# Batch 6's product with w made in fp32 between the counts and the matrix, and the matrix made by chunks

## The reference

```python
h = jnp.maximum(_layernorm(x, axis=-1), 0.0)           # x: (64, 128, 1024)
xp = jnp.transpose(h, (2, 0, 1)); n = 1024              # node, batch, feature
x_avg = xp.mean(axis=1)
x_norm = x_avg / jnp.maximum(norm(x_avg), 1e-12)
sim_flat = ((x_norm @ x_norm.T + 1.0) * 0.5).reshape(-1)
adj = (sim_flat + gumbel[:, 0] > 1.0 - sim_flat + gumbel[:, 1])   # n x n, 0 or 1
adj_sym = clip(adj + adj.T, 0, 1); nmask = clip(adj_sym + eye(n), 0, 1)
common = nmask @ nmask.T                                # the counts
struct = where(adj_sym * (common > 1) > 0, common / common.max() * common, 0)
W = adj * struct
dinv = where(W.sum(0) > 0, W.sum(0) ** -0.5, 0)
Wn = dinv[:, None] * W * dinv[None, :]                  # the matrix
xw = einsum('nbt,to->nbo', xp, weight)                  # each batch's product with w
out = x + transpose(einsum('sd,sbt->dbt', Wn, xw) + bias)
```

## Time and profile before

| | |
|---|---|
| median of 3 runs | 814.52 us (813.65 to 814.91) |
| profiled execution, its own time | 813.88 us |
| profiled execution, its span | 811.9 us |
| busy: PE, DVE, ACT, POOL | 97%, 68%, 62%, 37% |
| granted TensorE clock | 1.00 |

### The profile page before, as it was taken

One profiled execution on the slowest core, in us unless ns is written; L12 is line 12 of the kernel. 1 busy time (PEld: TensorE's weight loads), 2 busy tenths in 40 slices (PEclk: granted clock), 3 DMA queues, 4 the chain that ended last, 5 costly groups with the idle time before them and its releaser, 6 DMA issues.

```text
span 811.9 us, 14245 instructions
## 1 busy us (share of the span) xinstructions
PE 789.5 (97%) x5042; PEld 445.7 (55%) x5042; DVE 553.4 (68%) x668; ACT 502.3 (62%) x530; POOL 304.4 (37%) x389
## 2 busy tenths in 40 slices
PE   5999999899999999999999999999999999999998
PEld 5887766644455545554555455545555555545553
DVE  7999877999966656665666566656665666566653
ACT  4999966695665656655656565556664666566641
POOL 4667482103333333333333333333333333333320
PEclk9999999999999999999999999999999999999999
DMA  8999942005742223322322232223222322232112
GB/s 328 408 409 410 418 183 77 2 0 209 256 155 99 97 99 108 106 95 97 111 99 98 92 118 94 94 96 114 92 101 95 112 93 97 96 111 96 52 47 85
DMA packets 30126, 112.68 MB, mean 139 GB/s; under 512 B 3472, under 2 KB 3600, under 8 KB 29072
## 3 DMA queue, kind: packets, MB, share of 16 engines
q1 hardware_dynamic: 30096, 112.28, 38.0%
HBM read 78.71 MB, written 33.55 MB: 138 GB/s over the span
## 4 chain that ended last, share of the span: by engine, by line
PE 82%; DVE 3%; ACT 3%; issue 2%; POOL 1%; DMA 0%; POOLq 0%; DVEq 0%; ACTq 0%; SPq 0%
PE ps L998 67%; PE ps L915 8%; PE ps L1014 3%; PE ps L933 2%; DVE xring L1178 1%; ACT zbuf L492 1%; PE ps L785 1%; DVE a L1222 0%; ACT a L687 0%; PE ps L807 0%; PE ps L868 0%; DVE ybuf L1215 0%; ACT zbuf L561 0%; POOL zbuf L465 0%; DVE hring L1204 0%
## 5 line engine op out<-in xcount | busy, mean ns | idle before, releaser
L998 PE MATMUL ps<-a,ybuf 128*128 128x512 f16 x2604 | 570.8, 379 | 0.6 <-ACT obuf L598 0.3
L998 PEld LDWEIGHTS ps<-a,ybuf 128*128 128x128 f16 x2604 | 252.5, 98 | 296.4 <-issue 0.8
L1215 DVE TENSOR_TENSOR ybuf<-zbuf,ybuf 128x1024 f16<-128x1024 f32 x124 | 165.1, 1332 | 154.3 <-ACT ybuf L580 154.3
L463 POOL TENSOR_TENSOR zbuf<-zbuf 128x512 f32<-128x512 f32 x31 | 39.5, 1275 | 423.4 <-ACT zbuf L561 423.4
L580 ACT ACTIVATE ybuf<-zbuf 128x1024 f16<-128x1024 f32 x124 | 117.7, 950 | 114.3 <-POOL zbuf L468 98.9
L598 ACT ACTIVATE obuf<-ps,bias_sb,w_out 128x512 f32<-128x512 f32 x61 | 47.1, 772 | 111.9 <-PE ps L998 109.5
L1204 DVE TENSOR_TENSOR hring<-hring 128x1024 f16<-128x1024 f32 x53 | 67.0, 1264 | 54.7 <-ACT hring L539 54.7
L915 PEld LDWEIGHTS ps<-w,hring 128*128 128x128 f16 x1272 | 75.3, 98 | 12.6 <-issue 0.8
L915 PE MATMUL ps<-w,hring 128*128 128x128 f16 x1272 | 79.7, 219 | 0.3 <-DVE k L1248 0.3
L1374 DVE TENSOR_TENSOR obuf<-obuf,xring 128x1024 f32<-128x1024 f32 x63 | 77.2, 1226 | 2.7
L561 ACT ACTIVATE zbuf<-ps 128x1024 f32<-128x1024 f32 x55 | 56.3, 1023 | 22.0 <-PE ps L915 20.2
(11 more groups left out here) (164 smaller groups left out, 665.1 us busy)
## 6 DMA issues: line engine op xcount, KB each, us to landing
xring<-in_x_dram SPq DMA_DIRECT2D x96, 512.0 KB, 4.7
out_dram<-obuf SPq DMA_DIRECT2D x63, 512.0 KB, 2.9
ybuf<-in_x_dram SPq DMA_DIRECT2D x28, 512.0 KB, 11.9
a<-in_L_gnn_gumbel_dram SPq DMA_DIRECT2D x7, 1024.0 KB, 19.0
obuf<-in_x_dram SPq DMA_DIRECT2D x10, 512.0 KB, 6.0
obuf<-in_L_gnn_gumbel_dram SPq DMA_DIRECT2D x1, 1024.0 KB, 26.3
out_dram<-obuf SPq DMA_DIRECT2D x2, 256.0 KB, 2.1
w<-in_adj_dram SPq DMA_DIRECT2D x1, 64.0 KB, 1.9
```

Source lines behind the costliest of these rows:

```text
L998: mm = nc.tensor.matmul(bank[q % 2], y16[:, q % 2, yk, u, c * P:(c + 1) * P], a16[:, ak, mat, c, :], start=(start and c == yk == ak == 0), ...
L1215: nc.vector.tensor_tensor(y16[:, q % 2, 1, a:a + n, :], z[:, a + 1:a + 1 + n, :], y16[:, q % 2, 0, a:a + n, :], ALU.subtract).then_inc(s_y, 1)
```

## The change

1. Batch 6 is made as 4 and 5 are: `relu_first(6)` and `first_xw(6)`. `relu2(0, 3, 0)`, `h_low(0, 3, 0)` and `xw_of(0, 3, 0)` go.
2. Batch 4 goes to PSUM pair 3, batch 5 to pair 0, batch 6 to pair 3 again, once `z_of(0, 2, 0)` has read batch 4. The copy L675 goes; `z_of` reads the PSUM pairs, batch 4's before the first `square` and batch 5's behind it, not after the matrix. The eight matmuls of 4 and 5 are laid between `squared`, `q_row` and `turn`.
3. `y_low(0, 1, 2)` and `y_low(0, 1, 3)` go from VectorE to GpSimd, ahead of `roots`. `z_sums(2)` moves ahead to where `s_alo` reaches 10, the end of the parts of the first pair.
4. The first block of the matrix is handed over in four chunks of 128 rows instead of two of 256. `square` no longer scales; instead `high` scales by `kappa2` (kappa squared) and `low` multiplies and subtracts in one instruction. `top_of(1)` and the kappa steps stand behind one and two `rooted`.
5. L1332 waits for `first_xw(6)` and stands behind the last `low_part`, not before it. `partial(0, 2, 1)` stands ahead of `z_of(0, 3, 0)`; `partial(0, 2, 2)` waits for one store, `upper1(0, 2)` for the other.

The diff, cut to its core:

```diff
+        ps_early = {4: pair[3], 5: pair[0], 6: pair[3]}
-        EARLY = (1, 4, 5)
+        EARLY = (1, 4, 5, 6)
# GpSimd
             z_sums(1)
+            for g in (2, 3):
+                a, n = GROUPS[g]
+                pool.wait_ge(s_yhi, 4 + g + 1)
+                pool.wait_ge(s_y, 4 + 4 + g)
+                nc.gpsimd.tensor_tensor(y16[:, 1, 1, a:a + n, :], z[:, a + 1:a + 1 + n, :], y16[:, 1, 0, a:a + n, :],
+                                        ALU.subtract).then_inc(s_y, 1)
             roots(0, 0, HC)
             roots(1, HC, C)
-            with pool.Fori(2, TRIPS * PAIRS) as r:
+            pool.wait_ge(s_alo, 10)
+            z_sums(2)
+            with pool.Fori(3, TRIPS * PAIRS) as r:
# ScalarE
             relu_first(5)
-            act.wait_ge(s_xw2, 6)
-            nc.scalar.activation(xw_res[:, 0, :], ps_xw2, ACT.Copy).then_inc(s_spill, 1)
+            relu_first(6)
+            z_of(0, 2, 0)
-                nc.scalar.activation(r, r, ACT.Square, scale=kappa[:, 0:1]).then_inc(s_a32, 1)
+                nc.scalar.activation(r, r, ACT.Square).then_inc(s_a32, 1)
-                nc.scalar.activation(a16[:, 0, mat, :, :], src, ACT.Copy).then_inc(s_ahi, 1)
+                nc.scalar.activation(a16[:, 0, mat, :, :], src, ACT.Identity, bias=0.0,
+                                     scale=kappa2[:, 0:1]).then_inc(s_ahi, 1)
+            square(rows_hi, 0, 0, 0)
+            z_of(0, 2, 1)
+            square(rows_hi, 0, 0, 1)
+            act.wait_ge(s_kap, 4)
+            high_rows(0, 0, rows_hi, 0, 0, 1)
+            high_rows(0, 0, rows_hi, 0, 1, 2)
+            for c in (2, 3):
+                square(rows_hi, 0, 0, c)
+                high_rows(0, 0, rows_hi, 0, c, c + 1)
-            relu2(0, 3, 0)
-            z_of(0, 2, 0)
-            z_of(0, 2, 1)
             y_high(0, 2, 0)
# TensorE
+            pe.wait_ge(s_z, 4)
             for half in (0, 1):
+                first_xw(4, half, half + 1)
                 squared(C - 1, half).then_inc(s_diag, 1)
-            pe.wait_ge(s_z, 4)
-            first_xw(4).then_inc(s_xw2, 1)
-            stay_awake(ps[:, 1, 0:P], 2)
+            first_xw(4, 2).then_inc(s_xw2, 1)
+            first_xw(5, 0, HC)
             q_row(0)
+            first_xw(5, HC, HC + 2)
             turn(1)
+            first_xw(5, HC + 2).then_inc(s_xw2, 1)
             spread(1)
             q_row(1)
-            pe.wait_ge(s_spill, 1)
-            first_xw(5).then_inc(s_xw2, 1)
+            pe.wait_ge(s_z, 5)
+            first_xw(6).then_inc(s_xw2, 1)
                 product(1, 5, 5, ps_b, False)
-                xw_of(0, 3, 0)
                 pe.wait_ge(s_c, 14)
# VectorE
-            y_low(0, 1, 2)
             mask(5)
-            y_low(0, 1, 3)
             root(1, HC, C)
-            top_of(1)
             rooted(rows_hi, 0, 0, 0)
+            top_of(1)
+            rooted(rows_hi, 0, 0, 1)
...
+            nc.vector.tensor_tensor(kappa2[:], kappa[:], kappa[:], ALU.mult).then_inc(s_kap, 1)
+            rooted(rows_hi, 0, 0, 2)
+            rooted(rows_hi, 0, 0, 3)
+            low_part(0, 0, rows_hi, 0, 0)
+            low_part(0, 0, rows_hi, 0, 1)
+            rooted(rows_hi, 0, 1, 0)
+            low_part(0, 0, rows_hi, 0, 2)
+            rooted(rows_hi, 0, 1, 1)
+            low_part(0, 0, rows_hi, 0, 3)
...
+            low_part(3, 2, rows_lo, 1, 1)
+            dve.wait_ge(s_xw2, 8)
             nc.vector.tensor_tensor(spare, rows_hi[:, :, HI], rows_hi[:, :, LO], ALU.subtract).then_inc(s_t, 1)
-            low_part(3, 2, rows_lo, 1, 1)
-            h_low(0, 3, 0)
             low(4, 3, spare)
```

More of the change, by code:

```diff
@@ L118, in gnn_kernel @@
         kappa = sb("kappa", [P, 1])
+        kappa2 = sb("kappa2", [P, 1])
         w_out = sb("w_out", [P, 1])
@@ L601, in act_pair @@
             def act_pair(i, q, ahead1, ahead2):
+                first_loop = isinstance(i, int) and i == 0 and q == 2
                 partial(i, q, 0)
+                if first_loop:
+                    partial(i, q, 1)
                 if ahead1:
@@ L605, in act_pair @@
                     y_high(i, q + 1, 0)
-                partial(i, q, 1)
+                if not first_loop:
+                    partial(i, q, 1)
                 if ahead2:
@@ L693, in first_out, with high_rows @@
                                      scale=w_out[:, 0:1]).then_inc(s_first, 1)
-            for n, (mat, rows, k, half) in enumerate(((0, rows_hi, 0, 0), (A12, rows_hi, 0, 1),
-                                                      (1, rows_lo, 1, 0), (2, rows_lo, 1, 1))):
-                for part in (0, 1):
[L698 to L703, removed]
+            def high_rows(n, mat, rows, half, a, b):
+                act.wait_ge(s_a32, HC * n + b)
+                nc.scalar.activation(a16[:, 0, mat, a:b, :], rows[:, a:b, half * H:(half + 1) * H],
+                                     ACT.Identity, bias=0.0, scale=kappa2[:, 0:1]).then_inc(s_ahi, 1)
+            square(rows_hi, 0, 0, 0)
[7 more added lines that the diff above has]
+                high_rows(0, 0, rows_hi, 0, c, c + 1)
+            for n, (mat, rows, k, half) in enumerate(((A12, rows_hi, 0, 1), (1, rows_lo, 1, 0), (2, rows_lo, 1, 1))):
+                for part in (0, 1):
+                    square(rows, k, half, 2 * part)
+                    square(rows, k, half, 2 * part + 1)
+                    high_rows(n + 1, mat, rows, half, 2 * part, 2 * part + 2)
             act.wait_ge(s_wout, 1)
             act.wait_ge(s_bias, 16)
-            act.wait_ge(s_fh, 2)
+            act.wait_ge(s_fh, 3)
             first_out(0)
             first_out(1)
-            relu2(0, 3, 0)
             act.wait_ge(s_t, 1)
@@ L795, in _, with first_xw @@
             kept(TRIPS1 - 1, KEPT[1])
[L797 to L801, removed]
+            def first_xw(j, a=0, b=C):
+                pe.wait_ge(s_fh, j - 3)
+                for c in range(a, b):
+                    mm = nc.tensor.matmul(ps_early[j][:, c * P:(c + 1) * P], first_h[j][:, c * P:(c + 1) * P], w_unit[:],
                                           start=True, stop=True, skip_group_check=True)
@@ L1011, in first_pair @@
                             bank = FIRST_OUT[2 * (k % 2) + b][2]
-                            for c in (2 * part, 2 * part + 1):
+                            for c in cs:
                                 for yk, ak in ((0, 0), (0, 1), (1, 0)):
@@ L1017, in first_pair @@
                                                           skip_group_check=True)
-                            if part == 1 and k + b > 0:
+                            if cs[-1] == HC - 1 and k + b > 0:
                                 mm.then_inc(s_mm, 1)
@@ L1360, in upper1 @@
                 if isinstance(r, int) and r == 1:
-                    dve.wait_ge(s_hhi, 4)
+                    dve.wait_ge(s_hhi, before(0, BODY - 1) + 1)
+                if isinstance(r, int) and r == 2:
+                    dve.wait_ge(s_store[1], 32)
                 dve.wait_ge(s_mm, 14 + 7 * r + (6 if isinstance(r, int) and r == 1 else 5))
```

61 lines of the change are left out of this document (28 added, 33 removed).

## The result

| | before | after |
|---|---|---|
| median, 12 executions each on one chip | 814.48 us (813.51 to 815.42) | 815.91 us (814.65 to 816.89) |
| profiled execution, its own time | 813.88 us | 816.52 us |
| profiled execution, its span | 811.9 us | 814.7 us |

A forecast was written before the change was run, and what follows sets the result against it. TensorE was taken to bound the kernel: product(2, 5, 5) starts at 209.4 against 209.05, 0.35 us later, so 813.88 becomes 814.2, and 0.64 for the median gives 814.9. Own range 813.4 to 816.2; 8 in 10: 812.1 to 816.6.

The forecast's parts named there:

- End of the counts: Before the first product: powers 0.37 us earlier, q's maximum at about 149.8 for 150.3, GpSimd's two residues costing nothing.
- The rival in which the residues hold the masks: GpSimd's two residues keep masks 5 and 6 waiting, all up to q is late: 817.1 us; chance 0.10.
- New forms: VectorE's scaled subtraction in the matrix's parts costs 0.05 us more than the plain one, 2.51 a part.
- Turns: Second pair: four GpSimd sums alternate with VectorE's subtractions, putting 4 x 1.13 = 4.5 us into VectorE's list.
- first rival: Second pair: scaled subtractions take no turns with GpSimd's sums, or the sums lose every race: 812.3 us; chance 0.24.
- where the list starts: Second pair: VectorE ends low_part(3) at 171.2 and its list of subtractions follows from there.
- The xw's 1.34: TensorE, ahead of product(1, 2, 6): batch 6's f16 xw goes, yet that product starts 1.36 us later, at 195.1.
- hid a wait: Rival at product(1, 2, 6): the removed xw covered a wait, so its 1.34 us is no gain by itself; counted in the forecast.
- Old stalls: TensorE's two stalls between product(1, 2, 6) and product(2, 5, 5), 0.53 and 0.49 us, both go: 1.02 us.
- the clock: Rival: the clock falls in TensorE's new stalls of 2.5 and 1.2 us, twelve products cost 2.6 more: 817.5; chance 0.05.

The follow-up runs named there:

- e7: The kernel of e5 with the two y residues put back on VectorE: 812.10 us, ratio to before 0.9970.
- e3: The changed kernel with the four sums of z_sums(2) over 8 columns instead of 512: 811.75 us, ratio to before 0.9966.
- e1: The changed kernel with eight idle-keeping fp32 matmuls on TensorE ahead of the wait of product(1, 5, 5): 814.75 us, ratio to before 1.0003.
- e6: The kernel of e5 with batch 6's f16 xw back in the second pair: 812.20 us, ratio to before 0.9972.
- e5: The changed kernel with each sum of z_sums(2) held for one low_part (s_alo 5, 6, 7, 8): 812.08 us, ratio to before 0.9966.
- e2: The changed kernel with z_sums(2) held until low 6 is done (s_alo 13 for 10): 813.48 us, ratio to before 0.9989.
- e12: A second run of the kernel of e5, with the same edits: 812.33 us, ratio to before 0.9972.
- e8: The kernel of e5 with the matrix's first block in two halves again instead of four chunks: 813.26 us, ratio to before 0.9981.
- e11: A second run of the kernel of e8, with the same edits: 813.41 us, ratio to before 0.9984.

## Why the prediction held, and where it was off

The forecast was 814.9 and no change beyond 0.2%; 815.91 was measured, inside that and inside the range. Against before it said +0.4, measured was +1.4, which is 0.2 us short of the 1.6 that would have counted as a change. So the mechanism was right and the size was not, and that the result stayed inside is in part luck: an execution in which the clock falls is 2.5 us behind before by the times from M, and half of them had the fall. Step by step, times of after less 0.28 (its M stands 0.28 later):

- **End of the counts: nearly as forecast.** q's maximum was ready at 149.95 (forecast 149.8; 150.30 before, so 0.35 won and not 0.5), the powers started at 147.34 (147.24), the first product at 154.85 (154.85). GpSimd's two residues took 4.43 us and 1.91 of idle time still stood ahead of the powers, so they were hidden; the masks beside them kept 1.23. The rival in which the residues hold the masks is out, and e7 shows their move to be worth 0.33 us.
- **New forms: as forecast.** The scaled subtraction took 1.28 where the plain one took 1.22 (forecast 0.05 more), a part of the first pair 2.51.
- **Turns: as forecast, a tenth smaller.** Four turns of 1.0 us, not of 1.13: 4.0 us in VectorE's list, not 4.5. The scaled subtraction takes turns like the plain one (low 4 and low 5 at 3.36), which no row of before could show. The Trainium skill ("SBUF — State Buffer", Who interferes with whom) has it for every VectorE instruction with two SBUF inputs beside a GpSimd one that reads SBUF, and the trace agrees. That is the end of the first rival; e3 shows that its time would have been right (-1.97 for -2.2).
- **Mis-sized: where the list starts.** "VectorE ends `low_part(3)` at 171.2" was the step. L1362 started 38.32 after M, the forecast had it 37.43 after: 0.9 late. 0.68 of it is the bracket in after's row at 171.17: the last high half of ScalarE was not there. 0.15 was there already at the first part of `A12`, which ended at 160.15 for 160.0. I had costed VectorE's 2.51 and TensorE's 2.59 a part, and ScalarE's 2.2 only as a rate, not when its last part comes. From there to the end of low 7 the list took 22.4 us, forecast 22.5.
- **The xw's 1.34: in the sum as "hid a wait", and so it was.** At full clock VectorE's list decides that wait, as the prediction had it: in e1 `upper1(0, 1)` follows the lows without a bracket. In the profiled execution of after VectorE idles 1.38 ahead of it, at 196.80, since it also needs `product(1, 5, 5)` itself, which the low clock had let end only at 196.7. TensorE's stall ahead of `product(1, 2, 6)` was 0.90 there and 1.00 in e1, for 1.2. Without the xw every version has 0.9 us or more of idle time there; e6 puts the xw's removal at 0.35 us with the turns out of the way.
- **Old stalls: gone as forecast.** From `product(1, 2, 6)` to the end 617.09 us, 618.16 before: 1.07 for the 1.02 of the two brackets.
- **Wrong weight: the clock, by a row misread.** It was given 0.05, because 6.52 us of idle time near the start of before showed no fall in the page. Those rows are no case of a full clock that survives idle time. TensorE of before:

```profile
4.23 1.20 PE L754 MATMUL ps<-ones,zeros 128*128 128x128 f32 x4
11.95 3.75 PE L768 MATMUL ps<-w_unit,hring 128*128 128x128 f32 x16 [6.52 <-ACT hring L492]
...
16.65 1.95 PE L781 MATMUL ps<-w_unit,hring 128*128 128x128 f32 x16
```

  Sixteen such matmuls took 3.75 us behind the idle time and 1.95 from 16.65 on, and the four ahead of the idle time (1.20 us, where four take 0.61 at 149.95 in after) were as slow: TensorE ran at half its rate on both sides of the 6.52 us and reached the full one at about 16. The trace has no entry of the clock ahead of about 16 us, and the page reads 1.00 where it has none.
  In after the clock did fall, by its mean in six executions of twelve; the profile has it after 2.40 us of idle time, which were forecast at 2.5, and it cost 1.5 us at `product(1, 2, 6)` (63.56 against 62.06 in e1). The forecast price at half clock was 2.6; the twelve took 4.32 for 2.75, 1.57 more, because the clock came back before they were through. The Trainium skill ("TensorE: Matmul & The Clock Gate", HAM oscillation), which the prediction had set aside, was right to warn of idle time; this trace agrees.

Added up from M: 0.35 forecast, 0.9 for the late start of the list, 0.1 less for the list itself: 1.1, as e1 measured (+1.10). With the fall 2.5 (+2.52 in after's profile); half of the executions have it. The lowest executions of the two kernels, 814.65 and 813.51, differ by 1.1 as well. So one term was 0.9 us too small, and the one behaviour taken for unlikely came in half the executions, by their mean clock.

Where did the change's gain go? Alone, its parts bring 2.03 us (e5). 3.06 are given back because GpSimd's sums now start, by a hold at the tenth low half, exactly where VectorE's list of two-input instructions starts, and up to 1.5 by the clock in the stall that this makes. The hold itself decides: at 10 it costs 3.1 us over the best place (e1 against e5, the clock out of it), none at all costs 1.7, 13 costs 1.0, and 5 to 8 in steps costs nothing and is the fastest version that I have: 812.08 and 812.33 us, 2.6 and 2.1 under the medians of before beside them (814.69 and 814.45).

## What to carry to other kernels

When a change makes one engine earlier, look at what the other engines then have beside each other: two streams of instructions that read two SBUF tensors each share out the time by whole instructions, and here a semaphore wait per instruction, which put GpSimd's beside VectorE's instructions with one PSUM input, cost nothing. An engine's work that is removed from the place of a wait is worth only what stands out over that wait. And before a stall of some 2 us on TensorE is called cheap, add what the clock takes behind it in part of the executions, or fill it. A page's clock in tenths of a long slice is no proof that the clock held: look at a short window, and at the time that one matmul takes.

## What the hardware showed that I had not expected

- **The turns are strict.** VectorE's instructions were ready back to back, and still each waited for a whole sum of GpSimd, four times in a row; per turn VectorE lost 1.0 us (3.24 to 3.36 for 2.29 and 2.35), GpSimd 2.0 (3.21 to 3.33 for 1.27). Even sums over 8 columns (e3) took 6.93 us for four, since each still waited for one of VectorE's.
- **The clock's fall is not a fixed thing.** Counted by the mean granted clock (0.998 or less), it came in 6 of 12 executions of after, whose profile has 2.40 us of idle time there, and in 4 of 12 of e2, with 1.98; in e3 to e12, whose profiles have 1.23 or less once the program is under way, and in e1, it came in none. It went to 0.50 for about the next seven matmuls. What decides between executions of one kernel no run here shows.
- **A pause at the end.** The kernels with two halves (e8, e11) have 0.38 us more ahead of VectorE's last instruction, though TensorE ends no later, and lose 0.38 more behind it, both times, and the others not. The cause is open.
